# Ternary weights from ScalarE's sign and a minimum, and loads rearranged at both ends of a transformer layer

## What is computed

```python
x = layernorm(x + attention(x))            # x: 4 x 1024 x 512
x = layernorm(x + ffn(x))

# attention: 16 heads, 4 KV heads, each head with two halves of 32 (q1,q2,k1,k2), rotary
a1 = softmax(q1 @ k1.T * scale + causal); a2 = softmax(q2 @ k2.T * scale + causal)
out = (a1 - lam * a2) @ v                  # lam from four short lambda vectors
out = group_norm(out) * gn_w + gn_b        # per head and position
attention = out.reshape(B, T, 1024) @ Wo * (1 - LAMBDA_INIT)

def ternary_quant(w):                      # of W_up, W_gate, W_down: 2048 x 512 each
    scale = mean(abs(w)) + 1e-8
    return clip(round(w / scale), -1, 1) * scale
ffn(x) = (silu(x @ up.T) * (x @ gate.T)) @ down.T
```

## Time and profile before

| what | us |
|---|---|
| median of 3 runs | 2399.93 (2399.42 to 2401.19) |
| the profiled execution | 2401.43 |
| its span, first to last instruction | 2399.5 |
| PE busy in it | 2241.2 |
| DVE, ACT, POOL busy | 1797.6, 1457.2, 1260.2 |
| mean granted TensorE clock | 0.984 of full speed |

### The profile page before, as it was taken

One profiled execution on the slowest core, in us unless ns is written; L12 is line 12 of the kernel. 1 busy time (PEld: TensorE's weight loads), 2 busy tenths in 40 slices (PEclk: granted clock), 3 DMA queues, 4 the chain that ended last, 5 costly groups with the idle time before them and its releaser, 6 DMA issues.

```text
span 2399.5 us, 41382 instructions
## 1 busy us (share of the span) xinstructions
PE 2241.2 (93%) x13602; PEld 1397.6 (58%) x13602; DVE 1797.6 (75%) x3830; ACT 1457.2 (61%) x3530; POOL 1260.2 (53%) x1907
## 2 busy tenths in 40 slices
PE   7889989889899999999999999999899999999998
PEld 4556656555556666666665666666566666644444
DVE  3587898989887878887878888887777888832343
ACT  1467756464666767777666767777667767721232
POOL 0455688888664455554544555665544445521232
PEclk9999999999999999999999999999999999999999
DMA  6766655565643131312253312222342111013000
GB/s 224 221 195 217 202 176 180 176 185 171 185 137 102 45 93 58 98 54 68 87 157 94 93 54 84 80 84 63 106 119 80 49 45 62 28 56 112 1 18 18
DMA packets 257603, 256.53 MB, mean 107 GB/s; under 512 B 31344, under 2 KB 199408, under 8 KB 255216
## 3 DMA queue, kind: packets, MB, share of 16 engines
q1 hardware_dynamic: 246016, 220.26, 30.4%
q10 hardware_dynamic: 11376, 33.63, 4.3%
HBM read 182.53 MB, written 71.30 MB: 106 GB/s over the span
## 4 chain that ended last, share of the span: by engine, by line
PE 66%; DVE 14%; issue 7%; POOL 7%; ACT 2%; DMA 2%; SPq 0%; ACTq 0%; DVEq 0%; POOLq 0%
PE F L992 15%; PE PV L934 9%; PE F L979 9%; PE F L1001 8%; PE S L917 8%; PE F L962 7%; PE F L902 6%; DVE e_long L1245 4%; DVE e_long L1326 2%; PE PV L937 2%; DVE e_short L1326 2%; POOL x_lo L1218 2%; POOL linv L1175 1%; DVE e_short L1245 1%; PE F L970 1%
## 5 line engine op out<-in xcount | busy, mean ns | idle before, releaser
L1175 POOL TENSOR_TENSOR linv<-lsum,powers 128x2 f32<-128x2 f32 x512 | 412.9, 806 | 671.1 <-ACT e_long L1053 550.7
L1053 ACT ACTIVATE e_long<-e_long,nmax 128x768 f32<-128x768 f32 (+3 forms) x512 | 504.8, 988 | 156.0 <-DVE nmax L1245 152.3
L1245 DVE CUSTOM_DVE_ANT_0 e_long<-S,mask_b 128x768 f32<-128x768 f32 (+3 forms) x512 | 512.6, 1019 | 102.0 <-PE S L917 99.1
L917 PE MATMUL S<-kstk,qstk 128*128 128x384 f32 (+5 forms) x1536 | 505.4, 421 | 52.9 <-DVE nmax L1245 41.2
L917 PEld LDWEIGHTS S<-kstk,qstk 128*128 128x128 f32 x1536 | 278.0, 194 | 190.8 <-DVE nmax L1245 76.0
L1046 ACT ACTIVATE dt_long<-F 128x512 f32<-128x512 f32 (+3 forms) x512 | 239.4, 511 | 194.6 <-PE F L902 188.5
L1326 DVE SCALAR_TENSOR_TENSOR e_long<-e_long,coef 128x1024 f32<-128x1024 f32 (+3 forms) x256 | 308.9, 1207 | 49.9 <-POOL coef L1176 49.1
L1053 ACT ACTIVATE e_short<-e_short,nmax 128x384 f32<-128x384 f32 (+3 forms) x512 | 284.0, 558 | 50.5 <-DVE nmax L1245 49.0
L962 PE MATMUL F<-xT,wr 128*128 128x512 f32 x640 | 308.6, 615 | 4.1 <-issue 1.3
L1245 DVE CUSTOM_DVE_ANT_0 e_short<-S,mask_b 128x384 f32<-128x384 f32 (+3 forms) x512 | 237.9, 486 | 52.4 <-PE S L917 49.7
L979 PE MATMUL F<-wo_sb,at_sb 128*128 128x512 f32 x512 | 240.0, 603 | 15.9 <-issue 15.9
(11 more groups left out here) (107 smaller groups left out, 3361.8 us busy)
## 6 DMA issues: line engine op xcount, KB each, us to landing
qstk<-dq SPq DMA_DIRECT2D x512, 128.0 KB, 2.8
dq<-hl SPq DMA_DIRECT2D x32, 1024.0 KB, 5.0
wr<-in_w_proj ACTq DMA_DIRECT2D x48, 512.0 KB, 4.2
kstk<-dk SPq DMA_DIRECT2D x64, 256.0 KB, 5.5
da<-ra SPq DMA_DIRECT2D x32, 512.0 KB, 3.1
at_sb<-da SPq DMA_DIRECT2D x32, 512.0 KB, 4.2
x<-in_x SPq DMA_DIRECT2D x16, 512.0 KB, 6.1
dk<-hl SPq DMA_DIRECT2D x8, 1024.0 KB, 4.9
```

The costliest lines, as they stand in the source:

```text
L917: last = nc.tensor.matmul(slot[:, h, :], qstk[:, duo % 4, 2 * r + m, :].bitcast(F32R), kstk[:, g % 2, m, h * w:(h + 1) * w].bitcast(F32R), ...
L1053: nc.scalar.activation(e, e, ACT.Exp, bias=nmax[:, u % 8:u % 8 + 1], scale=-1.0, accum_out=lsum[:, n % 4, m:m + 1]).then_inc(s_exp, 1)
L1175: link(nc.gpsimd.tensor_tensor(linv[:, a % 8, :], lsum[:, a % 4, :], mone, ALU.pow))
L1245: nc.vector.tensor_tensor_reduce(out, slot, mask, -1.0, -NEG, ALU.add, ALU.min, nmax[:, u % 8:u % 8 + 1]).then_inc(s_negmax, 1)
```

## The change

Five things, in the order of the program.

1. **The start.** SP loads tiles 0 to 3 of x; tiles 4 to 7 wait until the second tile has been transposed. The first `x1` loads leave the start: they stand in SP's order after score step 100. ACT issues tiles 12 and 13 of x and the first `wr`, then copies; the second `wr`, the rotary table, the lambda vectors and `gn` are issued between and after the first four copies. The lambda sums on DVE and their exponent on ACT become pieces of the order (`lambda sums`, `lambda`) and follow these loads.
2. **Ternary weights.** ACT takes the sign of (weight + half the scale), in place of POOL's comparison; DVE takes the minimum of (weight > half the scale) and that sign, in place of a difference. `thr` keeps only the positive halves.
3. **Wo.** The last batch has a home of its own, `wo_late`, in the memory of `xT` and `wr` (which the projection no longer needs), loaded once the last projection job is filled. The other batches keep `wo_sb` as it was.
4. **Residual x1.** Stores of the output count in two semaphores, one for each half of a batch; the half of `x1` whose four output tiles are stored can be loaded.
5. **The order's rules.** SP's pieces get a cost (0.45 to 1.9 us, before 0.06), which moves pieces on all engines; and PE waits for the reader of its last small sum also ahead of the next small sum, not only ahead of the next product with v.

```diff
-            "hidden low": 1.32, "rsqrt": 1.5, "rotate": 2.9, "low": 2.6, "group": 2.9, "less": 2.9}.get(what, 0.06)
+            "load q": 1.0, "load k": 1.9, "load first": 0.5, "load x1": 0.5, "load wo": 0.48, "load a": 0.5, "store v": 0.45,
+            "store rotated": 0.45, "store a": 0.45, "store out": 0.5, "load weight": 0.5, "load v": 0.5, "load lambda": 0.8, "lambda sums": 0.5,
+            "hidden low": 1.32, "rsqrt": 1.5, "rotate": 2.9, "low": 2.6, "group": 2.9, "side": 1.1}.get(what, 0.06)
...
     elif what == "load wo":
-        out = [ITEM("fill", y_last(a - 1), 1) if a else ITEM("ternary", PREP - 1)]
+        out = [ITEM("fill", PROJECTION[-1], 1) if a == B - 1 else ITEM("fill", y_last(a - 1), 1) if a else
+               ITEM("ternary", PREP - 1)]
     elif what == "load x1":
-        out = [ITEM("store out", y_last(a - 1))] if a else []
+        out = [ITEM("store out", JOB("y", a - 1, b // 2, 1, 3)) if a else ITEM("scores", 100, 1)]
...
             def load_wo(b, c):
+                if b == B - 1:
+                    if c == 0:
+                        sp.wait_ge(s_ffull, INDEX[PROJECTION[-1]] + 1)
+                    sp.dma_start(wo_late[:, c, :], wo[c * P:(c + 1) * P, :]).then_inc(s_wo_late, 16)
...
             def load_x1(b, k):
-                if k == 0 and b:
-                    sp.wait_ge(s_out, 16 * NT * b)
+                if k % 2 == 0 and b:
+                    sp.wait_ge(s_out[k // 2], 16 * 4 * b)
...
                 if what == "load first":
+                    if a >= 4:
+                        sp.wait_ge(s_ffull, INDEX[X_JOBS[1]] + 1)
                     sp.dma_start(x_first[:, a, :], x_tiles[a]).then_inc(s_xfirst[a], 16)
...
-            load_w(0)
-            act.dma_start(cs[:, :, :], rope).then_inc(s_cs, 16)
-            load_w(1)
-            act.dma_start(lamv[:, :, :, :], lams_in.rearrange("(o a) b d -> o a b d", o=1)
-                          .broadcast_to((P, 2, 2, DH))).then_inc(s_lamin, 16)
-            act.dma_start(gn_sb[:, :, :], gn).then_inc(s_gn, 16)
...
+                elif what == "side":
+                    if a == 0:
+                        act.wait_ge(s_thr, 1)
+                    act.wait_ge(s_wt[a % 4], 16 * (PREP // 4 + a // 4 + 1))
                     if a >= 2:
-                        load_w(a)
+                        act.wait_ge(s_tern, a - 1)
+                    nc.scalar.activation(x1_lo[:, a % 2, :], wt[:, a % 4, :], ACT.Sign, bias=thr[:, a // 8:a // 8 + 1])\
+                        .then_inc(s_side, 1)
...
-                    dve.wait_ge(s_neg, a + 1)
-                    nc.vector.scalar_tensor_tensor(dst, wt[:, a % 4, :], thr[:, w, 0:1], x1_lo[:, a % 2, :],
-                                                   ALU.is_gt, ALU.subtract, saturate=False).then_inc(s_tern, 1)
+                    dve.wait_ge(s_side, a + 1)
+                    nc.vector.scalar_tensor_tensor(dst, wt[:, a % 4, :], thr[:, w:w + 1], x1_lo[:, a % 2, :],
+                                                   ALU.is_gt, ALU.min, saturate=False).then_inc(s_tern, 1)
```

More of the change, by code:

```diff
@@ L168 @@
 LANDS = {"load q": 3.1, "load k": 5.5, "load v": 4.5, "store v": 3.9, "store rotated": 5.2, "store a": 3.5, "load a": 4.4,
-         "store out": 2.5, "load wo": 4.0, "load x1": 6.0, "load weight": 4.5, "load x": 3.7, "load w": 4.2, "load first": 2.5}
+         "store out": 2.5, "load wo": 4.0, "load x1": 6.0, "load weight": 4.5, "load x": 3.7, "load w": 4.2, "load rope": 6.0, "load lambda": 5.0, "load first": 2.5}
 def width(n):
@@ L276, in after @@
         last = W_LAST[a - 2]
-        out = [ITEM("fill", last, PIECES[last.kind] - 1)] if a >= 2 else []
+        out = [ITEM("fill", last, PIECES[last.kind] - 1)] if a >= 2 else [ITEM("copy", X_JOBS[0])] * a
+    elif what == "load first":
+        out = [ITEM("fill", X_JOBS[1], 0)] if a >= 4 else []
+    elif what in ("load rope", "load lambda"):
+        out = [ITEM("copy", X_JOBS[1 if what == "load rope" else 3])]
+    elif what == "lambda sums":
+        out = [ITEM("load lambda")]
+    elif what == "lambda":
+        out = [ITEM("lambda sums")]
     elif what == "minus lambda":
@@ L291, in after @@
             u = ROT[JOB("O", a.b, a.h, a.i, a.j)]
+            out.append(ITEM("load rope"))
             if u:
@@ L322, in after @@
     elif what == "ternary":
-        out = [ITEM("less", a)]
+        out = [ITEM("side", a)]
     elif what == "factor":
@@ L396 @@
             [ITEM(what, c) for c in range(CHUNKS) for what in ("moments", "spread", "deviation")],
-            [ITEM("minus lambda")], [ITEM("all sums"), ITEM("scales"), ITEM("constants")],
+            [ITEM("lambda sums"), ITEM("minus lambda")], [ITEM("all sums"), ITEM("scales"), ITEM("constants")],
             [ITEM("ternary", i) for i in range(PREP)]],
@@ L415 @@
 AHEAD = {"minimum": 1.0, "exponent": 1.0, "evict": 1.5, "inverses": 1.0, "factor": 2.0, "combine": 0.6, "empty": 3.0, "copy": 2.0,
-         "sum": -1.5, "ternary": -1.5, "less": -2.0, "rsqrt": 1.0, "product": 0.5, "load q": 2.0}
+         "sum": -1.5, "ternary": -1.5, "side": -1.0, "rsqrt": 1.0, "product": 0.5, "load q": 2.0}
 NTH = 4
@@ L503, in choose @@
                     continue
-                other = None
-                if item.what in READER:
-                    other = ITEM("product", at["pe"][2] - 1)
-                elif item.what == "values" and small:
-                    other = ITEM(READER[small.what], small.a)
-                if other and other.a >= 0:
-                    if other not in end:
-                        continue
-                    r = max(r, end[other])
+                others = []
+                if item.what in READER and at["pe"][2]:
+                    others.append(ITEM("product", at["pe"][2] - 1))
+                if (item.what in READER or item.what == "values") and small:
+                    others.append(ITEM(READER[small.what], small.a))
+                if any(other not in end for other in others):
+                    continue
+                r = max([r] + [end[other] for other in others])
                 if item.what == "scores" and item.a and item.b == 0:
@@ L614, in layer_kernel @@
         xs = sb("xs", [P, 2, D])
+        with ExitStack() as once:
+            wo_late = once.enter_context(nc.sbuf_tensor("wo_late", [P, 8, D], F32))
         xT = sb("xT", [P, DC, BANK])
@@ L888, in _ @@
                     load_weight(a % PREP, a >= PREP)
-            sp.wait_ge(s_out, 16 * NT * B)
+            for half in range(2):
+                sp.wait_ge(s_out[half], 16 * 4 * B)
         @block.tensor
@@ L1009, in _ @@
             for what, a, b in ORDER["pe"]:
-                if what in READER:
-                    if made:
+                if what in READER or what == "values":
+                    if last_small:
+                        small, c = last_small
+                        pe.wait_ge({"mean": s_rv, "variance": s_gve, "totals": s_kk}[small], c + 1)
+                    last_small = None if what == "values" else (what, a)
+                    if made and what != "values":
                         pe.wait_ge(s_pvfree, made)
-                    last_small = what, a
                 if what == "scores":
```

66 lines of the change are left out of this document (33 added, 33 removed).

## The result

The changed kernel takes 2375.5 us (median of 4 runs, 2373.5 to 2379.4) against 2400.05 us (2399.4 to 2401.2) of the kernel before: a ratio of 0.9899, 95% interval 0.9882 to 0.9916. The forecast was 2368 us with a range of 2352 to 2383. Direction and range held; of the 32 us in the sum, 24.5 came. The profiled execution is the slowest of the four: 2379.4 us, span 2377.6.

The account below looks back on a forecast made before the run. TensorE, busy 2241.2 of 2399.5 us, was taken as the bound, with gains only from its idle time and low clock. Terms 5.5 + 12 + 3 + 11.5 = 32 us gave 2368 us, range 2352 to 2383.

Parts of the forecast that it names:

- Start: First x tiles to first projection product: copies no longer wait for lambda vectors, product at about 11.3 us, 5.5 us gained.
- Last batch: Between last `y` and Wo near 2154 us: idle 9.43 us and 2.0 us of low clock go, 11.5 us gained.
- Change of batch: At 1725 to 1740 us: work moved ahead of the first `wo` fills TensorE's 5.88 us wait, 3 us gained.
- Ternary stretch: 300 to 620 us: sign on ScalarE relieves GpSimd, TensorE idle near 8%, 12 us gained.
- The relief of GpSimd: 300 to 620 us: without comparisons GpSimd's busy time falls from 272.3 to about 200 us, 63%.
- New waits: Ternary pieces on ScalarE: the sign's waits for loads would be at most 6.5 us, beside 143 us of idle time.
- The reading that a combine is longer the fuller GpSimd is: VectorE's combine takes 1.27, 1.13, 0.90 us at GpSimd 85%, 58%, 54% busy; about 1.16 at 63%, saving 7.8 us.
- the rival of 26 us: Ternary stretch: GpSimd's relief is worth more, 26 us gained there, 2354 us in all; chance 0.17.
- The slower rival: Ternary pieces: each sign pushes its 1.06 us onto the exponents' path, 25.4 us lost, 2405 us; chance 0.04.
- A sign of being wrong: Ternary pieces: TensorE waiting for exponents behind signs on ScalarE would show the forecast wrong; no size given.
- The reordering takes back: Rest of the program: new order, same work, 6 us more idle or the start lost, 2374 us; chance 0.10.

Follow-up runs that it names:

- e7: Kernel before with only the new order of the first loads: 2396.0 us, ratio 0.9975.
- e6: Kernel before with only Wo's own home for the last batch and x1 loaded in halves: 2392.9 us, ratio 0.9961.
- e14: Changed kernel, computing engines' order kept, the 24 second weight loads up to 6 us of planned time earlier in SyncE's queue: 2362.8 us, ratio 0.9835.
- e3: Changed kernel without the second loads of the 24 weight pieces (wrong weights), every order kept: 2363.9 us, ratio 0.9840.
- e12: Changed kernel with only the 24 signs moved to GpSimd's queue as comparisons, all other order kept: 2403.5 us, ratio 1.0005.
- e1: Changed kernel with the comparison back on GpSimd and the difference on VectorE, planned anew: 2384.4 us, ratio 0.9928.
- e13: e1 with its order kept and only the 24 comparisons made signs in ScalarE's queue: 2380.2 us, ratio 0.9908.

## Why the prediction was right, and where its terms were off

**Start, 5.5 us: right.** The first rows in order of time:

```profile
4.29 1.08 PE L978 MATMUL F<-ident,wt 128*128 128x128 f32 x4 [4.29 <-DMA wt<-in_x]
...
8.03 2.24 PE L978 MATMUL F<-ident,wt 128*128 128x128 f32 x8 [1.08 <-DMA wt<-in_x]
...
10.31 0.60 ACT L1098 ACTIVATE xT<-F 128x512 f32<-128x512 f32 x1 [0.53 <-PE F L978]
...
11.00 9.28 PE L985 MATMUL F<-xT,wr 128*128 128x512 f32 x15 [0.73 <-issue]
18.20 0.69 DVE L1302 SCALAR_TENSOR_TENSOR t<-F,cs 128x512 f32<-128x512 f32 x1 [18.20 <-DMA cs<-in_rope]
```

The first product starts at 11.00, where 11.3 was forecast and 16.79 stood in the earlier trace rows; the table lands at 18.2 (forecast 17) and the lambda sums run on VectorE at 19.4, early enough. Alone (e7) the part brought 5.3 us.

**Last batch, 11.5 us: right.** TensorE and SyncE in order of time, to hold against the earlier trace rows:

```profile
2137.72 4.70 PE L1027 MATMUL F<-down_t,hid 128*128 128x512 fp8e4 x21
2142.25 27.63 PE L1005 MATMUL F<-wo_late,at_sb 128*128 128x512 f32 x64
2169.72 0.60 PE L1009 MATMUL F<-ident,x 128*128 128x128 f32 x4
```

No gap, and 64 products in 27.63 us (forecast 27.7, before 29.71): 9.4 + 2.1. The lead rises by 11.6 there, and by 11.4 in e6.

**Change of batch, 3 us: too high.** The loads of Wo are issued from 1721.03 on, the first product starts at 1731.84:

```profile
1728.74 0.33 PE L940 MATMUL S<-kstk,qstk 128*128 128x128 f32 x1 [0.46 <-DMA wo_sb<-in_wo]
1731.84 6.02 PE L1005 MATMUL F<-wo_sb,at_sb 128*128 128x512 f32 x8 [2.78 <-issue]
```

The idle time in front of it is 2.78 us instead of 5.88, so the reading of the row was right. But shorter waits of 0.37, 0.89 and 0.46 us now stand ahead of it (0.20 and 0.50 before), the window is busy for only 1.9 us more than before (15.34 against 13.43), and the lead gains about 1.4 from 1700 to 1800. e6, where the old order still stands at this place (5.75 us idle), gains nothing there. So the gain came from the work that the new order puts into the gap, as forecast, at half the size.

**Ternary stretch, 12 us: the sum nearly came, by two errors.** The lead rose by 10.4 us from 300 to 700 us, but only by about 5 up to 620 us, where the forecast's stretch ends, and TensorE idled 12.2% of it and not 8.4%. The relief of GpSimd was what was said: 201.4 us (forecast about 200), and line 1346, the combine, was even shorter than the 1.16 us forecast. Busy time and count in the stretches of the earlier trace rows:

```profile
120.00:300.00 180.00, 48.06 (x45) 0.99 0.65 202
300.00:620.00 320.00, 82.94 (x75) 0.96 0.60 186
620.00:2100.00 1480.00, 344.87 (x384) 1.00 0.28 84
```

That is 1.106 us against 1.268. The reading that a combine is longer the fuller GpSimd is holds for this stretch, but not as a rule by shares: from 120 to 300 us it fell from 1.131 to 1.068 us, while GpSimd's busy time rose from 104.55 to 112.28. The term that was mis-sized stands under "New waits": "on ScalarE the same waits would be at most these 6.5 us". They were 21.3 us, and by e14 and e3 they cost 12 to 15 us at the end. Two pairs bear on what sets such waits: with the loads in the same places GpSimd waited for 10.3 us (e12) where ScalarE waited for 21.3, and in e1's order GpSimd waited for 6.9 us (e1) and the signs, 1.8 us later in the plan, for nothing (e13). So the time between a load and its reader counts, and not the engine alone. The planner put the sign at the time when a 4.5 us landing would have been over, on the engine that holds the exponents. That GpSimd, busy for 85% of the time before, came late to its comparisons and so found most weights landed is my reading; no run shows it by itself. With the waits gone the same order gains 17.9 us (e14) to 21.9 us (e3) from 300 to 700 us. That lies between the forecast and the rival of 26 us, and e14's 2362.8 us lies in the same way between forecast and the rival's 2354. For the stretch itself the 12 us were about right without the waits: in e14 the lead rises by about 12 from 300 to 620 us (TensorE idle 9.7%), against about 5 in the changed kernel. The other error is what nobody priced: some 5 to 6 us gained from 620 to 700 us, in the changed kernel as in e14 and e3. Neither e13, with signs in e1's order, nor e12, with the comparison in the changed kernel's order, gains anything there, and what releases them is open. The two errors nearly cancelled, and that is luck.

**Combines beside GpSimd.** In the changed kernel the rotary work of GpSimd still meets the combines. In order of time, GpSimd and VectorE:

```profile
332.15 2.37 POOL L1234 TENSOR_TENSOR hl<-t,hl 128x1024 f32<-128x1024 f32 x1
...
332.47 2.74 DVE L1346 SCALAR_TENSOR_TENSOR e_long<-e_long,coef 128x640 f32<-128x640 f32 x1
```

The combine of 640 columns ends 0.69 us after the GpSimd instruction and took 2.74 us; the shortest of its group took 0.875 us. The Trainium skill (SBUF — State Buffer, "SBUF: two separate sides") lets such a pair hold the port in turn, and this row agrees. The 26 us that the rival drew from it were not reached even without waits.

**The slower rival** ("the sign holds up the exponents") named the right place and the wrong cause. A sign takes 1.15 us and hardly delays anything by that; its wait for weights does, by 0.89 us per piece on average and 0.5 us per piece at the end of the program. A sign of being wrong that the prediction named came in this form: in the example above TensorE stood for 4.29 us for a row minimum that had waited behind the sign's select. Its price was overrated because it supposed that GpSimd's relief was worth nothing.

**"The reordering takes back"** was priced at 6 us either way. In this kernel it took 8.5 us between 1200 and 1700 us; e3, e14 and e12, which keep the same order on the computing engines, lose 6.3 to 7.3 us in that stretch, and e1 and e13, which share another order, 3.4 and 2.7. So this loss belongs to the order. It lies between 1200 and 1600 us, where TensorE is busy for 380.8 us and was for 388.0. Two redraws that change no work cost 13 and 21 us. The bound should have been 10 to 20 us, and the range wider by it. That the forecast lay within 8 us of the result is partly luck.

What stays open: why one order is better than another between 1200 and 1700 us. The waits of TensorE from 1200 to 1600 us are many and below 2 us each, the largest group of them for VectorE's minimum (6.0 us in 12 waits against 4.4 in 10 before). And the three parts, each put alone into the kernel before, sum to 5.3 + 8.4 - 6.0 = 7.7 us instead of 24.5. The fifth item of the change, SyncE's costs in the planner and TensorE's further wait, is in none of them and was never run alone. Orders that differ by 10 us and more are enough to explain the difference, but no run splits it further.

## What to carry to other kernels

When an operation moves to another engine, price its waits by what stands behind it on the new engine, and its operand's arrival by the slowest landing behind its neighbours in the queue, not by the median; then issue the load earlier before anything else. Where a planner draws the order, measure an edit with the order held still as well, and redraw the order once with no edit, to learn how much of a difference is the draw. A price found in one order (4 to 5 us) can be five to seven times as large in another.

## What the runs showed of the hardware

- A sign of 128x1024 f32 into f16 with its bias from a tile took 1.135 to 1.165 us on ScalarE (24 of them in the changed kernel); the absolute value of the same piece with its sum took 1.05 us. Sign and exponent caused no further table load: the program has one. The estimate of 1.13 us drawn from the Trainium skill (ScalarE: Activation LUTs, "What ACT_TABLE_LOAD costs") holds.
- The same 512 KB load took 4.9 us at the median and 11.3 us behind four loads of k and a store on the same queue.
- The comparison on GpSimd takes 2.84 us at the median, up to 3.83 (e12), two and a half times the sign.
